# A layer norm in the pipeline's first phase: four blocks of x normed on ScalarE instead of VectorE

## The reference

```
x = u
x = x + 0.5 * ffn(layernorm(x))
x = x + attn(layernorm(x))
x = x + 0.5 * ffn(layernorm(x))

layernorm(x) = (x - mean) / sqrt(var + 1e-5)          # over the 128 features
ffn: shared = silu(x @ Ws_up) @ Ws_down
     aff = x @ centroids.T;  top 8 of 64 experts by aff + bias
     w = sigmoid(aff of the chosen) / their sum
     out = shared + sum over all 64 experts e of w[e] * (silu(x @ W_up[e]) @ W_down[e])
attn: xf = u @ WB.T, xb = u @ WBf.T (first and last token kept); gamma = sigmoid(xf @ w1 + xb @ w2 + b)
      out = gamma * (xf + xb) + (1 - gamma) * u
```

## Time and profile before

| | |
|---|---|
| median of 3 runs | 808.44 us (808.37 to 808.47) |
| the profiled execution | 808.82 us, its span 806.9 us |
| busy in the span | PE 796.3, DVE 659.6, ACT 627.3, POOL 424.3 us |
| granted TensorE clock | 1.00 of full speed in each stretch that was looked at |
| table loads on ScalarE | 1 |

### The profile page before, as it was taken

How to read it: one execution, slowest core, us unless ns; L and a number is a source line. 1 busy time by engine, 2 the same in 40 slices (tenths; PEclk the granted TensorE clock), 3 DMA queues, 4 the chain that set the end, 5 groups by cost and what they waited for, 6 DMA issues and landing times.

```text
span 806.9 us, 12441 instructions
## 1 busy us (share of the span) xinstructions
PE 796.3 (99%) x3671; PEld 648.4 (80%) x3671; DVE 659.6 (82%) x1426; ACT 627.3 (78%) x1207; POOL 424.3 (53%) x378
## 2 busy tenths in 40 slices
PE   7999999999999999999999999999999999999998
PEld 5787878888888888888888888888888888888786
DVE  6887989779797788977879779797898788787875
ACT  5987777778877778868787678787788787786885
POOL 3885546454555554545545455464554545454453
PEclk9999999999999999999999999999999999999999
DMA  7100000000000000000000000000000000000000
GB/s 258 33 1 13 14 1 1 0 20 8 14 1 0 26 0 13 0 0 26 0 13 0 0 26 0 13 0 0 26 0 0 0 2 27 0 1 1 14 0 14
DMA packets 15901, 11.44 MB, mean 14 GB/s; under 512 B 1664, under 2 KB 14848, under 8 KB 15872
## 3 DMA queue, kind: packets, MB, share of 16 engines
q1 hardware_dynamic: 15872, 11.08, 4.4%
HBM read 8.98 MB, written 2.10 MB: 14 GB/s over the span
## 4 chain that ended last, share of the span: by engine, by line
PE 92%; DVE 3%; ACT 2%; POOL 2%; DMA 1%; SPq 0%; issue 0%; DVEq 0%
PE y_ps L772 14%; PE y_ps L774 14%; PE up L773 14%; PE up L772 14%; PE up L774 14%; PE y_ps L773 14%; PE side L781 3%; PE side L791 2%; PE side L813 1%; PE side L812 1%; POOL g_lo L362 1%; ACT g_hi L481 1%; ACT up L447 1%; DMA wu_raw<-in_w_up 1%; DVE gated L635 0%; DVE g_lo L644 0%
## 5 line engine op out<-in xcount | busy, mean ns | idle before, releaser
L362 POOL TENSOR_TENSOR g_lo<-gated,g_hi 128x512 fp32r<-128x512 f32 x256 | 333.6, 1303 | 339.9 <-ACT g_hi L481 339.1
L447 ACT ACTIVATE up<-up 128x512 f32<-128x512 f32 x513 | 300.2, 585 | 87.4 <-PE up L774 85.4
L635 DVE TENSOR_TENSOR gated<-up,cw 128x512 f32<-128x512 f32 x256 | 175.3, 685 | 85.0 <-ACT up L447 80.2
L772 PE MATMUL y_ps<-g_hi,wd_hi 128*128 128x512 f32 x512 | 207.5, 405 | 1.0 <-POOL g_lo L362 0.9
L772 PE MATMUL up<-x_hi,wu_hi 128*128 128x512 f32 x512 | 202.4, 395 | 0.8 <-POOL wu_lo L369 0.7
L773 PE MATMUL up<-x_lo,wu_hi 128*128 128x512 f32 x512 | 202.5, 396 | 0.0
L774 PE MATMUL y_ps<-g_hi,wd_lo 128*128 128x512 f32 x512 | 202.5, 396 | 0.0
L774 PE MATMUL up<-x_hi,wu_lo 128*128 128x512 f32 x512 | 201.8, 394 | 0.0
L773 PE MATMUL y_ps<-g_lo,wd_hi 128*128 128x512 f32 x512 | 201.5, 393 | 0.0
L635 DVE TENSOR_TENSOR up<-up,cw 128x512 f32<-128x512 f32 x256 | 176.5, 689 | 23.8 <-ACT up L447 18.7
L481 ACT CAST g_hi<-up 128x512 fp32r<-128x512 f32 x256 | 151.1, 590 | 45.5 <-DVE up L635 42.4
(11 more groups left out here) (114 smaller groups left out, 504.3 us busy)
## 6 DMA issues: line engine op xcount, KB each, us to landing
x_in<-in_x SPq DMA_DIRECT2D x8, 256.0 KB, 2.8
wu_raw<-in_w_up SPq DMA_DIRECT2D x4, 512.0 KB, 6.2
wd_raw<-in_w_down SPq DMA_DIRECT2D x4, 512.0 KB, 7.0
x_res<-in_x SPq DMA_DIRECT2D x8, 256.0 KB, 2.7
out<-out_sb SPq DMA_DIRECT2D x7, 256.0 KB, 2.2
out<-out_sb SPq DMA_DIRECT2D x2, 128.0 KB, 1.8
ident<-in_ident SPq DMA_DIRECT2D x1, 64.0 KB, 2.4
sm_raw<-in_ws_up SPq DMA_DIRECT2D x2, 32.0 KB, 2.3
```

The source lines that it names most:

```text
L362: nc.gpsimd.tensor_tensor(g_lo[:, i, :], gated[:, t // 2 % ORING, :], g_hi[:, i, :].bitcast(fp32), ALU.subtract).then_inc(lo_done[1], 1)
L447: nc.scalar.activation(up[i][:, :], up[i][:, :], ACT.Silu).then_inc(silu_done, 1)
L635: nc.vector.tensor_tensor(gated[:, t // 2 % ORING, :] if t % 2 else up[i][:, :], up[i][:, :], cw[ph.q][:, :], ALU.mult).then_inc(gate_done, 1)
L772: nc.tensor.matmul(o, a[0], b[0], start=start, stop=False)
```

## The change

In phase 0 the norm of the next x moves from VectorE to ScalarE. ScalarE has one operation that computes func(scale * x + bias) with scale and bias per partition. With scale = rstd and bias = -mean * rstd, Identity gives the norm. The bias needs a small instruction of its own on VectorE ("shift", 128x4), in slot 10 between gate 10 and gate 11; it waits for rstd. ScalarE issues the four Identity activations of 128x128 in slot 11, behind Silu 11 and the high part of tile 10, ahead of Silu 12. The last one raises norm_done[0] as before. The other norms, in all later phases and the very first one ahead of phase 0, stay on VectorE. One small tile (128x4) and one semaphore are new.

```diff
 AT_FIRST = {
...
-    "stat0": (7, 8), "aggr0": 8, "rstd0": 9, "norm0": (11, 12),
+    "stat0": (7, 8), "aggr0": 8, "rstd0": 9, "shift0": 10, "norm0_act": 11,
...
+        shift = sb("shift", [P, NB])
...
+                    if ph.at.get("norm0_act") == t:
+                        act.wait_ge(x_in_done, 16 * (ph.norm0 + 1))
+                        act.wait_ge(shift_done, 1)
+                        for m in range(NB):
+                            made = nc.scalar.activation(normed[0][:, m, :], x_in[:, m, :], ACT.Identity,
+                                                        bias=shift[:, m:m + 1], scale=rstd[0][:, m:m + 1])
+                        made.then_inc(norm_done[0], 1)
...
+                    if ph.at.get("shift0") == t:
+                        dve.wait_ge(rstd_done[0], ph.norm0 + 1)
+                        nc.vector.scalar_tensor_tensor(shift[:, :], mv[0][:, :, 0], -1.0, rstd[0][:, :],
+                                                       ALU.mult, ALU.mult).then_inc(shift_done, 1)
```

More of the change, by code:

```diff
@@ L237, in build @@
         x2_done, kept_done, out_done = sem("x2_done"), sem("kept_done"), sem("out_done")
-        held, power_set = sem("held"), sem("power_set")
+        held, power_set, shift_done = sem("held"), sem("power_set"), sem("shift_done")
         norm_from = [x_in, x1, x2]
```

## The result

The changed kernel takes **812.17 us** (812.07 to 812.34, six runs) against 808.44 (808.37 to 808.47): 3.73 us more, ratio 1.0047 with a 95% interval of 1.0034 to 1.0060. The forecast was 808.1 us with a range of 807.0 to 808.9, and a chance of 0.06 for slower by over 0.2%. It missed, on one of the two sides that it held least likely (faster by over 0.2% had 0.06 as well).

What follows compares the result with a forecast made beforehand. GpSimd's hand-over to TensorE at 61.60, paced through ScalarE, was taken to bound phase 0. Waits removed 1.67, less shift 0.1 and norms 1.48, plus 0.28, gave 0.37 us: 808.44 to 808.1 us, range 807.0 to 808.9.

Steps and rivals of the forecast that it cites:

- carried to the end of the span unchanged: TensorE loses under half a microsecond from 62 to 800 us, so only phase 0 can win or lose time.
- TensorE's hole of 1.85 us: Phase 0, 32.30 to 34.15: TensorE waits for VectorE's norm; rival: paid back in full, 806.6 us, chance 0.06.
- What would show it: Expected trace: no norm wait, last TensorE wait on GpSimd some 1 us, norms 0.37 us apart, no second table load.
- The norm on ScalarE: Four Identity activations of 128x128 ahead of Silu 12, 0.37 us each, 1.48 us together.
- The shift: VectorE's 128x4 instruction ahead of gate 11, over 0.5 us, ending by 30.1; delays ScalarE's norms by 0.1 us.
- high part 13: ScalarE's piece at 34.73 in phase 0: 1.67 - 0.1 - 1.48 = 0.09 us earlier than before.
- Silu 20: ScalarE's activation at 42.71 in phase 0, on the chain to GpSimd: 0.37 us earlier.
- The wait for TensorE there: ScalarE's recorded idle ahead of the Silu at 42.71, expected to vanish and add 0.28 us of gain.
- the other two waits: ScalarE's waits for gates 12 and 13, counted as 1.20 + 0.47 = 1.67 us and expected to go.
- The table load: Rival: Identity needs another ScalarE table, two loads around the norms, 810.6 us; chance 0.05.
- its turn to GpSimd's next piece: Rival: on VectorE the shift also waits for GpSimd's piece at 29.98, giving 809.3 us; chance 0.05.
- Operands per partition: Scale and bias on ScalarE's norms, 0.17 us per norm; rival: they cost nothing, 807.2 to 807.6 us, chance 0.13.

Runs made afterwards that it cites:

- pad_only: Kernel before plus one unused 128x4 tile where the change puts its shift tile, nothing else of the change; 812.62 us, ratio 1.0052.
- shift_last: The whole changed kernel with its shift tile allocated behind all other tiles, which keep their old places; 808.26 us, ratio 0.9998 to the kernel before.

## Why the prediction was wrong

**The step that failed** is the one ahead of the sum, that from 62 us on whatever TensorE wins or loses by the end of phase 0 "is carried to the end of the span unchanged", and with it "0.37 us" as the whole effect. It holds only if TensorE's pace stays. The change was taken part by part (four norms, a shift, a wait, SP's load), but its one new tile was never priced. With that tile behind all others the change measures 808.26 us, in the range and 0.2 from the forecast. A tile in its place costs 4.15 us (pad_only), 1.35 ns on each of 3072 matmuls. None of the rivals had this mechanism, and the 0.02 left "for what I don't see" was far too little. The count of matmuls in a stretch of the earlier trace rows held what was needed to see afterwards, not beforehand: no row of before says that another layout has another pace.

**What bounds the gain** was right. TensorE's hole of 1.85 us went (31.94 behind 31.70) and was not paid back, the last wait of the phase is on GpSimd, and it is longer, 0.54 us recorded. With the 0.44 us of this execution added back, the trace forecast in "What would show it" is there but for one point: the last wait was to be some 1 us long and is 0.54 as recorded, 0.71 by the spacing (60.76 instead of 60.05, 0.23 behind 59.82).

**The terms.** The norm on ScalarE: 0.37 us forecast, 0.39 measured (1.55 / 4); the estimate by the page ScalarE: Activation LUTs of the Trainium skill (section "What ACT_TABLE_LOAD costs") had been 0.386, and the trace agrees with it. The shift: 0.65 us, four times the reciprocal of the same size, and ending at 29.60, where GpSimd's low part of 28.07 ends too (29.58). So it did not run free, and ScalarE starts the norms 0.15 us later than it could (29.70 against 29.55, the old 29.99 less the 0.44 of this execution), forecast 0.1. At high part 13 ScalarE is level with before (34.30 against 34.73 less 0.44), forecast 0.09 ahead. At Silu 20 it is 0.40 ahead, forecast 0.37. The wait for TensorE there was worth 0.39, not 0.28: from the high part ahead of it to the Silu it was 0.87 us before (41.84 to 42.71) and is 0.48 now (41.39 to 41.87). The recorded idle leaves out the overlap with the instruction ahead, which the prediction had added to the other two waits and not to this one. That the sum comes out within 0.03 us is luck in part: the terms are off by 0.1 in opposite directions.

**The rivals.** The table load did not come: one load as before, as the trace of before spoke for. The Trainium skill's page ScalarE: Activation LUTs, section "Table sets: the hidden batching unit", has identity in every set, and the trace agrees. The shift did not lose its turn to GpSimd's next piece, which starts at 29.53. Operands per partition are not free: the norms start 0.39 us apart, where size alone would give 0.20 by the prediction's line. The hole was not paid back.

## What to carry to other kernels

A new tile is part of a change: where TensorE is the bound, an unused tile in the same place (pad_only) and the change with its tile allocated last (shift_last) separate the edit from its layout in two runs. Compare the number of matmuls in a long stretch, not TensorE's busy time, when a kernel is slower everywhere by a fraction of a per cent. And try the distance between the weights and the streamed operands on purpose: here 128 more bytes of padding were worth 14 us, nearly 40 times what was forecast for the change.

## What was not expected of the hardware

- The spacing of 128x512 matmuls (fp32r) hangs on the distance in bytes between weights and streamed operands in SBUF: with TensorE alone 232.4 ns in the old layout, 234.3 with 32 bytes more, 226.7 with 128 or 384 more (means over 280 us). The two fast distances are whole multiples of 256 bytes, and the four slower ones are not. That this is so for all multiples, and which accesses meet, was not tried. The Trainium skill's page SBUF — State Buffer, section "Who interferes with whom", lists TensorE's reads of weights and of the moving operand as independent ports and says that TensorE never waits on anyone. The runs here show a pace that depends on the distance between the two with no other engine at work, and they decide for this kernel.
- All tiles moved by 32 bytes together gave 808.46 us, so this place is as good as the old one. No other was tried.
- The effect has no simple sign or size: in the whole kernel g alone by 32 bytes gains 1.3 us, x and g by 32 lose 4.15, x alone by -32 loses 1.5, and the weights by 32, which is x and g by -32, lose 1.9. Why was not found.
